# Attention and expert block on one core: two heads of a quad take their key tiles half a batch apart

## The reference, cut to what matters

```python
q, k, v = x @ Wq, x @ Wk, x @ Wv
latent_kv = (k + v) @ W_down_kv
k_rec, v_rec = latent_kv @ W_up_k, latent_kv @ W_up_v
scores = einsum('bhqd,bhkd->bhqk', qh, kh) * scale
decay = exp(-LAMBDA_DECAY * TIME_STEP * abs(idx[:, None] - idx[None, :]))
attn = softmax(scores * decay, axis=-1)
out = einsum('bhqk,bhkd->bhqd', attn, vh)
x = layernorm(x + out @ Wo)
x = layernorm(x + ffn(x))
```

## Time and profile before

| what | before |
|---|---|
| median of 3 runs | 682.22 us |
| the profiled execution's own time | 683.37 us |
| its span, first to last instruction | 681.6 us |
| mean granted clock of TensorE | 0.988 of full speed |
| attention part, start of the first and of the last exponential | 14.2 and 520.3 us |
| exponentials (L819) | 512, mean 1046 ns |
| outputs (L991) | 2048 passes, mean 601 ns |
| scores (L975) | 1408 matmuls, mean 409 ns |
| fixes (L1453) | 256, mean 429 ns |

### The profile page before, as it was taken

One profiled execution on the slowest core, in us unless ns is written; L12 is line 12 of the kernel. 1 busy time (PEld: TensorE's weight loads), 2 busy tenths in 40 slices (PEclk: granted clock), 3 DMA queues, 4 the chain that ended last, 5 costly groups with the idle time before them and its releaser, 6 DMA issues.

```text
span 681.6 us, 12895 instructions
## 1 busy us (share of the span) xinstructions
PE 653.9 (96%) x4763; PEld 292.2 (43%) x4763; DVE 309.9 (45%) x1000; ACT 551.4 (81%) x646; POOL 274.1 (40%) x257
## 2 busy tenths in 40 slices
PE   8999989999999999999999999999999999899985
PEld 4223323333333333333333333333334988686643
DVE  5434323543444345534434362335343452276677
ACT  5788979999999999999999999999998443244235
POOL 3965505602440543056024545502552104636630
PEclk9999989999999999999999999999999999799989
DMA  5658982572374255337624584323446688742112
GB/s 165 214 189 297 372 350 93 201 261 105 111 249 157 93 201 176 118 97 259 216 95 143 179 288 142 105 88 115 150 139 195 186 261 258 227 122 81 40 51 66
DMA packets 73555, 116.82 MB, mean 171 GB/s; under 512 B 6608, under 2 KB 49168, under 8 KB 73488
## 3 DMA queue, kind: packets, MB, share of 16 engines
q1 hardware_dynamic: 54688, 101.93, 44.3%
q10 hardware_dynamic: 15728, 7.72, 3.9%
q0 software_dynamic: 3072, 6.30, 3.1%
HBM read 68.73 MB, written 48.76 MB: 172 GB/s over the span
## 4 chain that ended last, share of the span: by engine, by line
PE 79%; DVE 6%; ACT 5%; DMA 5%; issue 2%; POOL 2%; SPq 1%; ACTq 0%; DVEq 0%; POOLq 0%
PE ps L991 29%; PE ps L975 19%; PE ps L1125 7%; PE ps L913 5%; PE ps L1120 5%; ACT probs L819 4%; DMA keys<-stack_dram 3%; PE ps L1138 2%; PE ps L1140 1%; PE ps L1010 1%; PE ps L1045 1%; PE ps L1040 1%; DVE ps L1453 1%; PE ps L1042 1%; PE ps L1142 1%
## 5 line engine op out<-in xcount | busy, mean ns | idle before, releaser
L819 ACT ACTIVATE probs<-ps 128x1024 f32<-128x1024 f32 x512 | 480.2, 1046 | 21.6 <-DVE ps L1453 12.2
L991 PE MATMUL ps<-probs,V 128*18 128x512 f32 x2048 | 270.8, 601 | 0.5 <-ACT probs L819 0.4
L975 PE MATMUL ps<-queries,keys 32*128 32x512 f32 (+3 forms) x1408 | 181.3, 409 | 6.3 <-DMA keys<-stack_dram 4.4
L1453 DVE TENSOR_TENSOR ps<-ps,cpk 128x256 f32<-128x256 f32 x256 | 102.1, 429 | 126.6 <-PE ps L975 112.3
L975 PEld LDWEIGHTS ps<-queries,keys 32*128 32x128 f32 x1408 | 92.3, 182 | 150.3 <-ACT probs L819 87.6
L607 POOL TENSOR_TENSOR stage<-qk,rows_sb 128x512 fp32r<-128x512 f32 x32 | 40.8, 1274 | 123.2 <-DVE qk L1300 118.4
L869 ACT ACTIVATE probs<-ps 128x512 f32<-128x512 f32 x48 | 28.5, 596 | 61.9 <-PE ps L1125 26.3
L649 POOL DMA_INDIRECT sorted_dram<-xn,slots x48 | 47.1, 981 | 61.7 <-ACT probs L819 48.5
L1125 PE MATMUL ps<-xnT,stage 128*128 128x512 f32 x128 | 61.0, 610 | 0.0
L991 PEld LDWEIGHTS ps<-probs,V 128*18 128x18 f32 x2048 | 34.5, 96 | 55.8 <-issue 40.3
L1575 DVE TENSOR_TENSOR probs<-probs,ps 128x512 f32<-128x512 f32 x48 | 32.7, 686 | 51.6 <-PE ps L1120 13.8
(11 more groups left out here) (206 smaller groups left out, 591.6 us busy)
## 6 DMA issues: line engine op xcount, KB each, us to landing
stack_dram<-stage SPq DMA_DIRECT2D x60, 512.0 KB, 6.7
keys<-stack_dram SPq DMA_DIRECT2D x30, 512.0 KB
queries<-stack_dram SPq DMA_DIRECT2D x30, 512.0 KB
keys<-stack_dram SPq DMA_DIRECT2D x30, 256.0 KB
keys<-expert_dram SPq DMA_DIRECT2D x28, 192.0 KB
sorted_dram<-y_pre SPq DMA_DIRECT2D x1, 4096.0 KB, 18.4
rows_sb<-expert_dram SPq DMA_DIRECT2D x16, 192.0 KB
V<-expert_dram SPq DMA_DIRECT2D x16, 192.0 KB
```

The costliest lines, as they stand in the source:

```text
L819: nc.scalar.activation(probs[:, m % 3, 2 * j:2 * j + 2, :], ps[:, 2 * s:2 * s + 2, :], ACT.Exp, scale=SCALE).then_inc(exp_done, 1)
L975: last = mm(bank[2 * s + i][:, lo:hi], keys[rows, u, kt // CT, v, tok(kt % CT)], queries[rows, u, v, lo:hi], start=True, stop=True)
L991: last = mm(bank[OUT_BANK][32 * i:32 * i + 2 * (HD + 1), :], V[:, c // 2 % 2, kt, k + i, half * (HD + 1):(half + 2) * (HD + 1)], probs[:, ...
L1453: tt(d, d, diag_fix.unsqueeze(1).to_broadcast([P, 2, P]), ALU.mult).then_inc(diag_done, 1)
```

## The change

Past the first two quads (m >= 2 * NT) the third and fourth head of a quad take the key tile (m + 4) % 8 where the first two take m % 8. So every tile has one half with keys of the queries' own half batch, which may hold a diagonal, and one without. `half_of(n)` says which pair of heads the n-th half is: the pair without a diagonal goes first, which in tiles where the first two heads cross means that the pairs change places. The outputs of a head take the values of its key tile. The waits at the start of a quad and for a free buffer of probabilities go by the place of the half, no longer by the pair.

```diff
--- before.py
+++ after.py
@@ -239,9 +239,19 @@
         def crossing(c, kt):
             return kt // CT == c % 2
 
+        def key_tile(m, j):
+
+
+            return (m + CT * j) % NT if m >= 2 * NT else m % NT
+
+        def half_of(n):
+
+            m, j = n // 2, n % 2
+            return 1 - j if m >= 2 * NT and crossing(m // TPC, key_tile(m, 0)) else j
+
         crossings = [0]
         for n in range(2 * TILES):
-            c, kt = n // 2 // TPC, n // 2 % NT
+            c, kt = n // 2 // TPC, key_tile(n // 2, half_of(n))
             crossings.append(crossings[-1] + crossing(c, kt))
 
         def side_places(c):
@@ -809,10 +819,10 @@
             keep_xT(1, bank[SIDE_BANK])
 
             def exponential(n):
-                m, j, s = n // 2, n % 2, n % SLOTS
-                if m >= 3 and j == 0:
+                m, j, s = n // 2, half_of(n), n % SLOTS
+                if m >= 3 and n % 2 == 0:
                     act.wait_ge(pv_done, m - 2)
-                if crossing(m // TPC, m % NT):
+                if crossing(m // TPC, key_tile(m, j)):
                     act.wait_ge(diag_done, crossings[n + 1])
                 else:
                     act.wait_ge(scores_ready, n + 1)
@@ -953,16 +963,16 @@
 
             def scores(n):
 
-                m, j, s = n // 2, n % 2, n % SLOTS
-                Q, c, kt = m // NT, m // TPC, m % NT
+                m, j, s = n // 2, half_of(n), n % SLOTS
+                Q, c, kt = m // NT, m // TPC, key_tile(m, j)
                 u = Q % 2
-                if m % NT == 0 and j == 0 and Q >= 2:
+                if m % NT == 0 and n % 2 == 0 and Q >= 2:
                     pe.wait_ge(stack_loaded[u], 48 * (Q // 2))
                 if n in (0, 2):
                     pe.wait_ge(first_operands, n + 2)
                 if n == 2 * CT:
                     pe.wait_ge(side_kept, numbers["first", 4])
-                if j == 0 and m - NT in (0, 1, CT):
+                if n % 2 == 0 and m - NT in (0, 1, CT):
                     pe.wait_ge(side_kept, numbers["operand", {0: 1, 1: 3, CT: 4}[m - NT]])
                 if n >= SLOTS:
                     pe.wait_ge(exp_done, n - SLOTS + 1)
@@ -978,19 +988,19 @@
 
             def outputs(m):
 
-                Q, c, kt = m // NT, m // TPC, m % NT
+                Q, c = m // NT, m // TPC
                 half, k = Q % 2, quad(Q) % 2 * 4
                 if m == 0:
                     pe.wait_ge(first_v_kept, 2)
                 if m == CT:
                     pe.wait_ge(side_kept, numbers["v", 1])
-                if kt == 0 and half == 0 and Q:
+                if m % (2 * NT) == 0 and Q:
                     pe.wait_ge(o_evacuated, Q // 2)
                 pe.wait_ge(exp_done, 2 * m + 2)
                 for i in range(4):
                     last = mm(bank[OUT_BANK][32 * i:32 * i + 2 * (HD + 1), :],
-                              V[:, c // 2 % 2, kt, k + i, half * (HD + 1):(half + 2) * (HD + 1)], probs[:, m % 3, i, :],
-                              start=(kt == 0 and half == 0), stop=(kt == NT - 1 and half == 1))
+                              V[:, c // 2 % 2, key_tile(m, i // 2), k + i, half * (HD + 1):(half + 2) * (HD + 1)], probs[:, m % 3, i, :],
+                              start=m % (2 * NT) == 0, stop=m % (2 * NT) == 2 * NT - 1)
                 last.then_inc(pv_done, 1)
 
             count = [0]
@@ -1445,7 +1455,7 @@
 
             def fix_diagonal(n):
                 m, s = n // 2, n % SLOTS
-                c, kt = m // TPC, m % NT
+                c, kt = m // TPC, key_tile(m, half_of(n))
                 if not crossing(c, kt):
                     return
                 dve.wait_ge(scores_ready, n + 1)
```

## The result

The kernel after takes **687.54 us** (median of 20 runs, 681.07 to 695.77) against 682.30 for the kernel before beside it (20 runs); the ratio is 1.0069, 95% interval 1.0047 to 1.0092. That is 4.7 us slower by the ratio, with the whole interval on the slower side and its middle beyond 0.5%. The forecast was 680.3, no change, 675 to 685. The profiled execution took 690.36 us (span 688.6), 7.0 more than the one before.

What follows compares the result with a forecast made beforehand. ScalarE was taken to set the pace, waiting where TensorE has side work and falls behind. The terms -7.5 + 5.2 + 0.4 = -1.9 us, from 682.22, gave 680.3 us, range 675.0 to 685.0.

Steps and rivals of the forecast that it cites:

- the walk: Four timing rules from the timeline carried through tiles 36 to 255; last exponential at 518.8 us before, 1.5 short of the trace.
- Step 1: In front of first halves' exponentials: the diagonal fix leaves, and the gaps it ends go; gain 7.5 us.
- Step 2: Second half's fix: its exponential is ready before ScalarE is free for it; cost nothing, cover 0.44 us.
- Step 3: Side bank copies queue behind VectorE's fix, stalling TensorE's side pieces 0.20 to 0.88 us in 22 pairs; 6.2 us, 5.2 at the end.
- D: Side bank's copy waits for the fix's end, a pair stalls 0.30, the 7.5 are given back: 682.2 us; chance 0.15.
- C: Second half's fix starts later, at S+0.85 (S: scores' start), each pair stalls 0.50: slower, up to 686.5 us; chance 0.13.
- B: Stalls behind the side bank's copies do not bind; gain 7.5 less 0.4, 675.1 us; chance 0.22.
- Step 4: Tiles 16 to 33: tile 32 still waits for keys until 87.77, an earlier request lands no earlier; gain nothing there.
- Step 5: Loads of keys at chunks 2, 4 and 6: time from evacuation to landing kept, wait 0.3, no term of its own.
- the likeliest case: The forecast itself: gaps go, side bank stalls take most of it back, 680.3 us, own range 678.5 to 682; chance 0.50.

Runs made afterwards that it cites:

- after_third: The kernel after, unchanged, run again on the chip of the kernels with fillers: 683.61 us, 1.0058 of the kernel before.
- after_again: The kernel after, unchanged, run again on another chip than the first pair's: 672.65 us, 1.0024 of the kernel before.
- after_fill: The kernel after with 2 to 8 overwritten filler matmuls before the waits for keys at chunks 1, 2, 4 and 6: 669.41 us, 0.9995 of the kernel before.
- after_fill_again: The kernel after with the same filler matmuls before the waits for keys, measured again on another chip: 679.04 us, 1.0014 of the kernel before.
- before_again: The kernel before, unchanged, run again on the chip of other experiments: 671.36 us, 1.0005 of the kernel before.
- before_fill: The kernel before with the same filler matmuls before the waits for keys at tiles 32, 64, 128 and 192: 678.79 us, 0.9993 of the kernel before.
- before_ones: The kernel before, with second halves of tiles without a diagonal also multiplied by ones from tile 16 on: 678.67 us, 1.0118 of the kernel before.
- before_idle: The kernel before, with the scores of tile 64 also waiting for every exponential ahead of them: 671.92 us, 1.0018 of the kernel before.
- after_apart: The kernel after with side pieces moved so that most directly following ones come apart, without fillers: 666.67 us, 0.9959 of the kernel before.
- after_apart_fill_again: The kernel after with side pieces moved apart and filler matmuls before the waits for keys, measured again: 662.09 us, 0.9886 of the kernel before.
- before_behind: The kernel before with a fix-sized VectorE product into spare memory ahead of side bank copies in tiles without a fix: 684.47 us, 1.0207 of the kernel before.
- after_take_first: The kernel after with VectorE emptying the side bank ahead of the second half's fix: 672.96 us, 1.0033 of the kernel before.

## Where the prediction held, and where it failed

This table compares the start of the first exponential of tiles 40, 64, 72, 240 and 255 with the first trace of the kernel before; each entry is by how much a stretch grew (us). The first row is the author's working; on record is its sum of -1.9, and not how it is split.

| | 40 to 64 | 64 to 72 | 72 to 240 | 240 to 255 |
|---|---|---|---|---|
| the walk, for the change | +0.1 | +0.2 | -1.8 | -0.4 |
| after | +1.1 | +2.9 | +0.1 | +2.4 |
| after_third | +1.0 | +2.8 | 0.0 | -0.7 |
| after_again | +1.1 | +1.6 | -0.8 | -0.7 |
| after_fill | +0.7 | +0.3 | -0.9 | -0.7 |
| after_fill_again | +1.2 | +0.3 | -0.1 | -0.7 |
| before_again | +0.1 | 0.0 | -0.1 | 0.0 |
| before_fill | +0.6 | 0.0 | +0.2 | 0.0 |
| before_ones | +0.8 | +0.6 | +6.4 | 0.0 |
| before_idle | +0.9 | +0.9 | -0.2 | 0.0 |
| after_apart | +0.3 | +2.3 | -3.3 | -0.7 |
| after_apart_fill_again | +0.5 | -0.2 | -5.1 | -0.7 |

- **Step 1** (the fix leaves the first half) held: 6.7 us of gaps became 0.4, and with the order turned round 28.2 us came back. The 7.5 us were not measured alone.
- **Step 2** (nothing waits for the second half's fix) held: 0.4 us, once, in the traces of the kernel after and in that of before_ones.
- **Step 3** (the stalls) held in kind, and in size on TensorE: 5.4 us in 21 places, against 6.2 in 22. What they cost at the end is less sure: removing nearly all of them brought 4.9 to 6.3 us, against 5.2 in the walk, but bringing them in with the ones cost 7.8 in the trace, against 5.4. The rivals D and C named the same place with larger prices, and B said none. The rows speak against all three as mechanisms; the time at equal clock, below, does not tell D's "no difference" from the forecast. D hung on a copy that starts only at the fix's end. It starts 0.34 behind the fix's start, of 0.43. The Trainium skill, "VectorE: DVE Perf Modes", section "The DRAIN you can't avoid", which the prediction took as speaking for D, says in the same paragraph that a next operation that is not held starts earlier; the trace agrees with that.
- **Step 4** stays open. Tile 32 waits for its keys until 85.88, with 2.16 of idle, where the prediction had them as late as now (87.77) and called an earlier landing a sign of being wrong. But with the same code up to there the kernel before has them anywhere from 86.10 (before_idle) to 89.92 (before_again), and after_again has them at 88.98, so one pair of traces can't tell, and no run shows that an earlier request would land no earlier. For the same reason the table starts at tile 40. The clock falls behind this wait in both kernels: from 85 to 93 us it is 0.79 before and 0.57 after.
- **Step 5 failed**, and with it the sum. "In the walk the wait is then 0.3, no term of its own": the wait before tile 64 was 1.78, and 1.72 and 1.77 in the two repetitions. SyncE requests those keys behind stores that don't follow TensorE's pace, at 145.10 before and 145.23 after, so the 0.4 us that TensorE had gained by tile 56 were worth nothing there, and from request to first use it took 6.65 instead of 5.95 us. That is the +1.1 of the first column. Behind it the clock fell, which no step of the forecast had as a term: +1.6 to +2.9 in the second column. All four traces with the change and without fillers or a moved fix have that fall behind tile 64 (after, after_again, after_third, after_apart); the two of the kernel before and the six with fillers have none.
- The rest, tiles 72 to 255, was -1.5 and -1.6 in after_again and after_fill against -2.2 in the walk, and -0.7 to -0.8 in after_third and after_fill_again. In the traces of the first pair's chip and of the third batch's an idle of 0.7 to 1.0 us near tile 240 takes about 1 us of it away; in the first trace the clock fell behind it too, and the column shows +2.4 instead of -0.7.

The account for the profiled execution: +5.7 at the last tile (of it 1.1 wait for keys, 2.9 and about 3 for the two falls of the clock, -1.3 for all else) and +1.3 in the expert part, which is 163.4 us behind the last tile's exponential instead of 162.1. At equal clock the change is worth -0.9 (± 1.1) and -0.2 (± 1.4) us in the second and third batch: the forecast of -1.9 is just inside the first and just outside the second, and 0 is inside both. These hold the longer wait for keys, 1.0 to 1.1 in the table; without it they come near the forecast. So the engines' work went about as the likeliest case had it, as far as this can tell, though neither the gain nor the price in it was measured alone, and the walk may have both too small. The kernel was slower all the same, through a wait and a clock that were left out. The loss differs from chip to chip: 1.0069 and 1.0058 where the kernel before takes 682 and 679 us, 1.0024 where it takes 670.

**Open** is why the transfer for tile 64 takes 6.6 instead of 6.0 us after the change (it is 6.5 in before_fill and 6.6 in before_behind, and 6.2 in after_fill, so it is not the change's indices alone). This longer transfer is 0.70 of the 0.97 by which the idle at tile 64 grew, so why the wait got long is for the most part not shown. Open also is the idle near tile 240: scores start at 492.99 there, and both the exponential (494.79) and VectorE's fix (495.48) that wait for them come about a microsecond late.

## What to carry to other kernels

Taking a wait out of an engine's cycle moves work against its surroundings: ask where the engine waits next for something that does not follow its pace (here a load behind stores), for there the gain ends, and a longer idle can cost clock besides. Read each run's granted clock beside its time; the 5 us here were more clock than work. When a change moves a recurring operation, fit anew the places of what was laid out around it: the same change cost 2 to 5 us at the old places, and with new places and fillers it came out 5.2 and 7.7 us ahead of the kernel before as it is. Compare each kernel at its own best places: at the new ones the kernel before is worse, and the difference of 12.7 there flatters the change.

## What the hardware showed beyond expectation

- Whether TensorE's clock falls is not told by the length of one idle alone. Over all traces, from tile 32 to the end of the attention part, it fell behind every idle of 1.57 us or more (17 of them, up to 3.96). Of the 15 between 0.92 and 1.53 it fell behind three: 0.95 in after, 1.02 in after_apart and 1.36 in before_behind; it stayed up behind 1.53 in after_take_first. At tile 64 a fall cost 0.9 (before_idle) to 2.9 us (after), and the one near 498 us about 3.
- A product with both operands in SBUF on VectorE took 0.4 to 1.45 us, the long ones beside GpSimd's work, while a product of the same size in PSUM took 0.43 (one in before_behind and one in before_ones 0.64).
- Four matmuls of 0.26 us each in front of the wait at tile 64 left 1.03 us of idle in after_fill_again, and the clock stayed up in all six traces with fillers there. The mean clock of the runs went from 0.9836 to 0.9907, though single runs with fillers still have 0.986.
